# Decoder block, last phase: which product uses which pair of PSUM banks, and where the attention projection stands in TensorE's order

## The reference

```python
x1 = x + attn(...) @ Wout + bout                       # "attention projection"
Q  = layernorm(x1)                                     # q0 in the kernel
q  = layernorm(Q, ln1_g, ln1_b) @ wq                   # 16 heads of 64
qn = q / norm_per_head(q)
y  = Q + qn @ N + bo                                   # N per batch: context keys and values times wo
x2 = x1 + y + gelu(layernorm(y, ln2_g, ln2_b) @ w1 + b1) @ w2 + b2
out = x2 + gelu(layernorm(x2) @ T1 + fb1) @ T2 + fb2   # T1, T2 ternary
```

## Time and profile before

| | before |
|---|---|
| median of 3 runs | 1515.29 us (1514.23 to 1517.01) |
| the profiled execution's own time | 1514.44 us |
| its span | 1512.7 us |
| mean granted TensorE clock | 0.857 of full speed |
| matmul busy time | 1113.5 us, 74% of the span |
| VectorE busy time | 781.4 us, 52% |
| ScalarE busy time | 658.2 us, 44% |

### The profile page before, as it was taken

One profiled execution on the slowest core, in us unless ns is written; L12 is line 12 of the kernel. 1 busy time (PEld: TensorE's weight loads), 2 busy tenths in 40 slices (PEclk: granted clock), 3 DMA queues, 4 the chain that ended last, 5 costly groups with the idle time before them and its releaser, 6 DMA issues. The chain is left out here.

```text
span 1512.7 us, 22497 instructions
## 1 busy us (share of the span) xinstructions
PE 1113.5 (74%) x7045; PEld 808.3 (53%) x7045; DVE 781.4 (52%) x1374; ACT 658.2 (44%) x1130; POOL 320.8 (21%) x402
## 2 busy tenths in 40 slices
PE   4763438877887785457543669998999999999875
PEld 2432214433343331356442558787877778787764
DVE  4885437544664450354423346565565646573623
ACT  1333005544555465213220344656556474746432
POOL 1432445511222122100101022112120304040300
PEclk9776559988989898656755889999999999999987
DMA  2333431211111100312434020303030302010000
GB/s 76 101 105 105 132 104 60 87 58 57 57 56 57 58 32 19 110 52 118 167 133 120 0 98 2 110 0 111 0 111 0 97 14 97 14 55 15 1 15 14
DMA packets 57715, 99.14 MB, mean 66 GB/s; under 512 B 7417, under 2 KB 41985, under 8 KB 53569
## 3 DMA queue, kind: packets, MB, share of 16 engines
q1 hardware_dynamic: 55744, 92.48, 18.2%
q0 software_dynamic: 1920, 6.03, 1.3%
HBM read 62.45 MB, written 35.65 MB: 65 GB/s over the span
## 5 line engine op out<-in xcount | busy, mean ns | idle before, releaser
L663 DVE TENSOR_REDUCE p_mx<-p_psA 128x2 f32<-128x256 f32 (+3 forms) x256 | 204.6, 824 | 173.5 <-DVEq L662 170.5
L738 ACT ACTIVATE p_probs<-p_psS 128x512 f32<-128x512 f32 (+1 forms) x352 | 185.6, 559 | 232.3 <-ACTq L737 230.4
L760 PE MATMUL p_psA<-p_ks,p_qs 96*128 96x384 bf16 (+3 forms) x512 | 144.4, 335 | 57.3 <-PEq L756 55.9
L780 PE MATMUL p_psS<-p_qs,p_ks 99*128 99x256 bf16 (+3 forms) x512 | 128.4, 326 | 68.1 <-PEq L806 58.8
L1659 DVE TENSOR_TENSOR p_hl<-p_h,p_hh 128x512 fp32r<-128x512 f32 x128 | 87.0, 689 | 157.3 <-DVEq L1658 156.5
L698 POOL TENSOR_SCALAR_AFFINE_SELECT p_probs<-p_probs 128x512 f32<-128x512 f32 x128 | 81.1, 634 | 265.0 <-POOLq L697 245.8
L1544 ACT ACTIVATE p_h<-p_psG,w_columns 128x512 f32<-128x512 f32 x128 | 88.2, 689 | 101.4 <-ACTq L1543 101.0
L780 PEld LDWEIGHTS p_psS<-p_qs,p_ks 99*128 99x128 bf16 x512 | 45.1, 104 | 138.3 <-issue 126.1
L762 PE MATMUL p_psA<-p_mask_b,p_ident_b 128*128 128x128 bf16 x512 | 115.2, 242 | 0.0
L760 PEld LDWEIGHTS p_psA<-p_ks,p_qs 96*128 96x128 bf16 x512 | 54.7, 107 | 103.9 <-issue 89.2
L1870 PE MATMUL p_psY<-p_n,p_hh 128*128 128x256 f32 x512 | 104.6, 288 | 3.0 <-PEq L1930 2.8
(11 more groups left out here) (246 smaller groups left out, 2725.4 us busy)
## 6 DMA issues: line engine op xcount, KB each, us to landing
p_n<-n_parts SPq DMA_DIRECT2D x16, 1024.0 KB, 6.7
n_parts<-p_nh SPq DMA_DIRECT2D x8, 1024.0 KB, 3.9
n_parts<-p_nl SPq DMA_DIRECT2D x8, 1024.0 KB, 6.0
q_parts<-p_part SPq DMA_DIRECT2D x96, 64.0 KB
p_qs<-q_parts SPq DMA_DIRECT2D x32, 192.0 KB
o_sums<-p_o SPq DMA_DIRECT2D x128, 34.0 KB
p_x<-in_x_dram SPq DMA_DIRECT2D x8, 512.0 KB, 3.8
p_qs<-q_parts SPq DMA_DIRECT2D x32, 128.0 KB
```

What stands on the lines that cost most here:

```text
L663: nc.vector.tensor_reduce(mx[:, h:h + 2, i], psA[buf][:, :, 0:P * (i + 1)], AX_X, ALU.max).then_inc(A_free, 1)
L738: nc.scalar.activation(probs[:, g % 2, at:at + n * w], psS[(g * len(SUNITS) + s) % SB][:, 0:n * w], ACT.Exp, scale=SCALE).then_inc(exp_don ...
L760: nc.tensor.matmul(psA[buf][:, z, 0:n], qs[0:SROWS, k, h, i * P:(i + 1) * P], ks[0:SROWS, k, g, 0:n], start=True, stop=False)
L780: last = nc.tensor.matmul(bank[:, z * w:(z + 1) * w], key, qs[0:SROWS + MROWS, k, h, j * P:S], start=True, stop=True)
```

## The change

The cross product and the head sums now have one pair (pair 1), and M, T and the attention projection have the other (pair 0). In the loop's rounds the attention projection is issued after the rows of X0 instead of after the rows of M7; in the first round it stood after X0 already. No instruction is added or taken away.

```diff
-        M_PAIR, A_PAIR, X_PAIR, T_PAIR = 0, 1, 0, 1
+        M_PAIR, A_PAIR, X_PAIR, T_PAIR = 0, 0, 1, 0
...
-        sums = psY[2 * T_PAIR]
+        sums = psY[2 * X_PAIR]
...
             def head_sums(j):
                 if j == 0:
-                    pe.wait_ge(pair_free[T_PAIR], 1)
-                    pe.sem_inc(pair_free[T_PAIR], -1)
+                    pe.wait_ge(pair_free[X_PAIR], 1)
+                    pe.sem_inc(pair_free[X_PAIR], -1)
...
                         pe.sem_inc(rn_ready, -1)
 
-                        pe.sem_inc(pair_free[T_PAIR], 1)
+                        pe.sem_inc(pair_free[X_PAIR], 1)
...
                             finish(kind, m, (at + i - LAG) % LAG, more)
-                            if kind == M and m == XT - 1 and front and more:
-                                attention_rows()
-                            if kind == X and m == 0 and not back and more:
+                            if kind == X and m == 0 and more:
                                 attention_rows()
```

## The result

Over 22 runs the changed kernel has a median of 1523.64 us (1514.23 to 1526.52), the kernel before over as many runs 1514.47 us (1510.35 to 1522.02). The ratio is 1.0042, 95% interval [1.0026, 1.0058]: slower by 6.4 us, by that comparison between 3.9 and 8.8 (the two medians lie 9.2 us apart, the means 7.3). The profiled execution has a span of 1517.8 us at a mean granted clock of 0.858, where it was 1512.7 us at 0.857: 5.1 us more. The forecast was no change that can be told, +2.3 us, with an upper end at 1519.6 us; the median lies above it.

What follows compares the result with a forecast made beforehand. TensorE was taken to set the pace. Six loop rounds losing 0.38 us each gave +2.3 us, the seventh round 0: 1514.44 + 2.3 = 1516.7 us, or 1517.6 us against the median of 1515.29; range 1514.3 to 1519.6 us.

Steps and rivals of the forecast that it cites:

- 3.17 + 0.07: Loop rounds: projection's 3.17 us plus 0.07 restart after its wait, putting X3's spread at 1016.51, 0.64 us later.
- the range: Forecast time from 1514.3 to 1519.6 us: rival 2 less one microsecond, rival 1 plus half for spread of medians.
- X0 opens behind its own low half: Loop rounds: X0 behind M7 waits only for its low half, opening at about 1011.07 after 0.27 us idle.
- The projection opens 0.31 us behind M's readout: Loop rounds: the readout still ends at 1012.96, the projection opens at 1013.27, and TensorE idles another 0.23 us.
- X3 absorbs, 0.38 us reach the end: Loop rounds: X3's old wait absorbs part of 0.64 us; 0.38 lost per round, +2.3 us over six (1.2 to 3.8).
- the signs to look for: Loop rounds: 0.27 us before X0, 0.23 before the projection, X3's wait down from 0.23 to 0.1, rounds about 0.4 longer.
- The seventh round gains nothing: Seventh round: X0's 2.31 us wait turns into waits at X2 and X3; gain 0, with 2.2 us the other end.
- The other owners cost nothing: Head sums, M0 and T0 find their pairs freed early enough under the new allocation; no cost.
- Rival 1: At the projection's opening on M's pair: the full 0.64 us or more stays, 3.8 us, 1519.1 us; chance 0.22.
- Rival 3: Seventh round's 2.3 us come through by rotation: 1513.0 us, or about 1515.3 with the loop's loss; chance 0.10.

Runs made afterwards that it cites:

- the changed kernel's second profile: The changed kernel run again unchanged, against the kernel before: median 1520.24 us against 1517.38, ratio 1.0012.
- extra work of 0.47 us: The kernel before with the spreads of X1 and X2 issued twice in each of the six loop rounds: ratio 1.0015.
- the third: The changed kernel run a third time unchanged, against the kernel before: 1520.39 us against 1517.55, ratio 1.0021.
- The two half changes: The kernel before with only the projection moved behind X0 (1531.0 us, ratio 1.0086), or with only the pairs changed (1533.3 us, ratio 1.0102).
- the two repetitions: The changed kernel run twice more unchanged, against the kernel before: 1520.24 us (ratio 1.0012) and 1520.39 us (ratio 1.0021).
- the fastest kernel above: The kernel before with VectorE's inverse norms cut in two halves of columns and one unit earlier: 1502.48 us, ratio 0.9910.

## Why the prediction was wrong

The step that failed is the term "3.17 + 0.07" for the projection behind its wait: it took 3.38 us, which made six rounds lose 2.9 us instead of 2.3. A second term was missing, the last round, and the base of the range, three runs, was too small. The order of events in the rounds came out as forecast.

- *X0 opens behind its own low half*: right, but 0.15 us later than forecast, at 1011.22 instead of 1011.07. From the low half's end to the opening it took 0.45 to 0.48 us in every round of the three profiles, where the prediction had taken 0.30 from T0. The bracket of 0.27 us agrees with the forecast's 0.27 by luck: it counts from the end of the spread's record, while the forecast counts from the next possible start, and by that measure the idle time is 0.42. It cost nothing more, because the projection's opening doesn't hang on X0; that one's idle time shrank from the forecast 0.23 us to 0.10.
- *The projection opens 0.31 us behind M's readout, at 1013.27*: measured 1013.27. The readout doesn't move: right.
- *Projection 3.17 + 0.07 us, X3's spread 0.64 us late*: **this term failed.** It took 3.38 us, and the spread came 0.78 us late. Its opening cost 0.09 us more than without a wait (0.54 against 0.45 us to the first rows matmul; the sum had 0.07), and its 24 matmuls took 2.83 us instead of 2.72, 0.118 us apart instead of 0.113, for which the sum had nothing. I had carried over a duration from a stretch with no wait ahead of it. In four rounds of the changed kernel's second profile the 24 matmuls took 2.73 to 2.74 us behind the same wait, and there the loss was 0.35 to 0.39 us, the forecast's 0.38. Why the 24 matmuls take the one or the other time stays open.
- *X3 absorbs, 0.38 us reach the end*: 0.44 us at X3's rows, 0.47 to 0.52 us in the rounds. The absorbing is real (extra work of 0.47 us cost 0.20 to 0.26), but it is the same 0.2 to 0.3 us whatever comes, and the spread was 0.14 us later. X3's wait went to nothing, where the signs to look for had 0.1 us left of it. Six rounds gave 2.9 us (2.4 in the second profile, 2.9 in the third), not 2.3; inside the stated 1.2 to 3.8.
- *The seventh round gains nothing*: right, 20.48 and 20.49 us. The wait of 2.31 us was the most striking row of the profile and was worth nothing there, because X2's and X3's rows hang on VectorE and GpSimd. Only in executions in which the clock falls behind it, 3 of 8 profiles, does it cost 0.5 us; the prediction had no such term.
- *The other owners cost nothing*: right; no round shows a wait at the head sums or at M0.
- *Rival 1*, the full 0.64 us or more, overstates the rounds, though its total of 3.8 us lies nearest to the measured 3.7 to 4.7. *Rival 3*, the rotation, fell: the Trainium skill's rule (Perfetto Trace Analysis, "Optimizing Tensor Performance") has groups rotate through banks, and both kernels do: three products in a row have pairs 0, 1, 0. The two half changes don't, there the same pair is asked for by the product next behind M, and they lost 2.2 and 2.6 us a round; so far the trace agrees with the rule. Between the two kernels that rotate it doesn't choose. What decided was what stood between a pair's last rows and its next opening: the projection, 3.17 us, covers a readout that ends 2.4 us behind M7; X0, 1.97 us, doesn't.
- *The missing term*: nothing in the sum stood for the last round, in which TensorE waits 3.3 us and the clock stays low for 10.2 or 13.7 us. Over all profiles the stretch with the seventh and the last round goes from 100.1 to 102.2 us, and it was 1.1 us against the changed kernel.
- *The range*: its upper end allowed 0.5 us for the spread of medians, read off three runs that lay 2.8 us apart. Executions of the same kernel turned out to span 20 us, and medians of 12 to 35 runs of it 1514.5 to 1520.8 us. A median taken from three such runs is no base for an end at +4 us; the range needed several us more on either side. How far above it the first median came, at 1523.64 us, is in part scatter: the two repetitions had 1520.24 and 1520.39, just above the upper end.

## What to carry to other kernels

When two accumulations share a PSUM pair, compare two durations: the readout's end behind the last matmul, and the length of what stands in between. Order and allocation must be changed together: each half alone cost about five times as much as both. Add to the duration what a wait in front of it costs beyond the idle time: here 0.09 us at the opening, and in some rounds 0.11 us in the matmuls behind it. A long wait in a profile is worth what the next waiter behind it leaves: follow it one or two units on before counting it, and if an engine has one long operation in a stream of short ones that others wait for (here a reciprocal of 3.35 us, 1.75 us for each half), cut it and slip the short ones in between. For a fraction of a per cent, compare the start-to-start of repeated rounds in two traces (0.05 us apart here in one kernel, 0.13 in the other) rather than medians (several us).

## What the runs showed of the hardware

- The time of an execution follows the mean granted clock: a straight line through all timed runs, with a level of its own for each kernel, gives about 1.0 us for each 0.001, and the clock goes from 0.845 to 0.860. The loop rounds are at 1.00 throughout in the profiles of both kernels, so this comes from the other phases, the seventh round and the last.
- The clock can fall within a loop round: with 1.58 and 2.32 us of idle time about 5 us apart, two rounds of six had a stretch at the lower level (a clock of 0.72 over 6 us) and were 1.6 us longer than the other four; with 1.58 and 2.54 us two of six again. With 1.58 and 0.27 us it fell in none of the 18 loop rounds in the changed kernel's profiles. Behind the single wait of 2.31 us in the seventh round it fell in 3 of 8 profiles, in one of them, that of the fastest kernel above, with no wait at M5 before it.
- The same 24 matmuls of 256 columns, the projection's rows, take one of two times at a granted clock of 1.00: 2.72 to 2.74 us (0.113 to 0.114 us from start to start) or 2.82 to 2.84 (0.118). Opened without a wait they took the shorter time in 53 of 54 loop rounds of the 15 profiles, opened behind one in 14 of 34 (leaving aside the two with a low clock, where only the pairs were changed). The cause is not shown.
- How long TensorE starts behind a signal depends on what it waits for: 0.14 us behind the low half at X3's rows, 0.30 at T0's opening, 0.45 to 0.48 at X0's opening in the changed kernel, which waits for a low half, a load and the pair, one after the other. Why it is longer there was not tested.
